# Attention heads in groups of three and two, maxima in the score stack, division in token rows

## The chip, the core and the metric

The kernel runs on one core of a Trainium2 chip. The core has TensorE (PE, with its weight loads shown as PEld), VectorE (DVE), ScalarE (ACT), GpSimd (POOL) and SyncE (SP, which here only issues DMAs). The metric is the device time of one execution in microseconds (us), the median of several runs.

## The reference, cut to what matters

Two layers over 4 sequences of 512 tokens of width 128. Each layer is a gated cross-attention (16 heads of width 8, 77 keys, context of the same sequence) and then a gated mixture of 8 experts (layer 0 picks one expert, layer 1 two). Layer 0 rotates queries and keys, layer 1 has biases and a mask on the keys.

```python
q = (x @ Wq).reshape(B, Nq, H, hd).transpose(0, 2, 1, 3)      # H = 16, hd = 8
attn = jax.nn.softmax(jnp.einsum('bhqd,bhkd->bhqk', q, k) * scale, axis=-1)
out = jnp.einsum('bhqk,bhkd->bhqd', attn, v).transpose(0, 2, 1, 3).reshape(B, Nq, C) @ Wo + bo
...
x = x + jnp.tanh(g_xattn[0]) * _L0_xattn_ref(_layernorm(x, axis=-1), ctx_1024, ...)
x = x + jnp.tanh(g_ffn[0]) * _L0_ffn_ref(_layernorm(x, axis=-1), ...)
x = x + jnp.tanh(g_xattn[1]) * _L1_xattn_ref(_layernorm(x, axis=-1), ctx_1024, ctx_1024, mask_SxS2_ik0, ...)
x = x + jnp.tanh(g_ffn[1]) * _L1_ffn_ref(_layernorm(x, axis=-1), ...)
```

## The kernel before

**Order.** Every engine runs its own program, and each walks the same list of steps k (`STEPS`) for each layer; a stage of batch b is due at step 12 b + `AT[stage]` (`due`). Within a step the order of the calls is the order of the engine's loop. A batch has 12 score tiles (`NS`), so batch b's scores are at steps 12 b to 12 b + 11. The maxima of batch b come in steps -12 to -3 relative to its first score, so they run during the scores of batch b - 1; its division, projection, second normalisation and routing come in steps 13 to 35, so during the scores of later batches. The front of a batch (statistics, normalisation, projection of the queries) comes in steps -30 to -19, that of batch 1 at 6 instead of 12 steps after that of batch 0 (`SECOND_FRONT`). After the steps of a layer follow `plan` and the expert tiles (24 and 40 tiles of 128 rows, L813 to L846 on PE).

**Attention.** Heads go in 4 groups of 4. Queries and keys are split in a high and a low half so that one single-pass float32r matmul gives their product: a stack of 128 rows holds high and low queries (`qs`, L342) against high and low keys (`ks`). 32 rows of dimensions carry 4 heads; the keys of one head are zero in the rows of the other heads, so `ks` has 4 x 77 = 308 columns for a group and batch.
- `spread_q` (L332, SP): 16 DMAs a batch that copy 32 rows of `qhl` into rows of `qs`, after `qh_ok` and `ql_ok` (the high and low half, L516 on ACT and L1020 on DVE). Three `qs` buffers rotate.
- `scores_for_max` (L718, PE): 16 units a batch, one per group and tile of 128 tokens, token rows against 308 keys; in layer 1 a mask matmul first (L730). Results go through a ring of 3 PSUM banks that other small results share. `maxima` (L1022, DVE) reduces each unit to 4 negated maxima.
- `split_max` (L1028) splits the maxima in high and low, `augmenting` (L733) transposes them, `copy_augT` (L518, ACT) takes them out of PSUM.
- `scores` (L737, PE): 12 tiles a batch of 103 or 102 key rows x 512 tokens: one matmul of queries and keys (L750) and one that adds the negated maxima and, in layer 1, the mask (L751). `exps` (L524, ACT) writes the exponentials to `probs`; two PSUM banks alternate.
- `weigh` (L753, PE): three times a batch, after 4 tiles: 4 matmuls of values into `ps_n` and 4 of ones into `ps_d`, plain float32, each with 32 output rows.
- Division: copies of `ps_d` and `ps_n` (L535, L536, ACT), `den_to_tokens` (4 transposes), `recip_den` (DVE), `widen_rd` (L538, ACT), `rden_to_dims` (4 transposes), `weigh_out` (L1049, DVE), then `output` (L777, PE) and `residual`.
- Keys, for both layers during layer 0: `spread_keys` (L673, PE) stacks the halves in 4 pairs of matmuls over 2 PSUM banks, `take_keys` copies each out (two on ACT, two on DVE), `mask_keys` writes the 4 heads from the copies. Layer 1's keys are spread at step `LAST + 24`, one step ahead of the router of batch 3.

## Time and profile before

| | us |
|---|---|
| median of 3 runs | 451.59 |
| lowest and highest run | 450.32, 460.82 |
| span of the profiled execution | 464.2 |
| PE busy (share of the span) | 314.7 (68%) |
| DVE busy | 264.1 (57%) |
| ACT busy | 136.3 (29%) |
| POOL busy | 152.2 (33%) |

The profile is one execution, and longer than the median by 12.6 us, so durations below come from it and sums are made against its span. Layer 0's attention fills about 10 to 160 us, its expert tiles 160 to 210, layer 1's attention 210 to 365, its tiles 365 to 447, and the end adds the results. The granted clock of TensorE is given as a share of 2.4 GHz; it is either 1.2 or 2.4 GHz at any moment, and a share between is a mean of the two over the stretch. A row with "x4" merges four instructions in a row.

### The profile page before, as it was taken

The page shows a single profiled execution, that of the slowest core. Times are in us where ns is not written, and L with a number is a line of the kernel's source. Part 1 is how long each engine was busy: PE and PEld are TensorE (multiplying, and loading weights), DVE is VectorE, ACT ScalarE, POOL GpSimd, SP SyncE. Part 2 cuts the span into 40 slices and gives each one's busy share as a digit, 9 for nine tenths or more (in the row PEclk, how much of TensorE's full clock was granted, in tenths as well). Part 3 has the DMA queues.
Part 4 walks back from the last instruction along what each step waited for, and adds up shares of the span by engine and source line. Part 5 has one row for each costly group of instructions (what it writes and reads, how often), then busy time and mean ns, then how long its engine had stood idle before and what let it go on. Part 6 is the DMA issues. An engine that isn't in the chain of part 4 may idle for free.

```text
span 464.2 us, 7008 instructions
## 1 busy us (share of the span) xinstructions
PE 314.7 (68%) x1932; PEld 228.1 (49%) x1932; DVE 264.1 (57%) x916; ACT 136.3 (29%) x302; POOL 152.2 (33%) x172
## 2 busy tenths in 40 slices
PE   2468999989754095751467999999530298888920
PEld 2236555545353094640256566654320297777820
DVE  2768668773675244353367667765545066665634
ACT  2412354535313033220103454354200033333300
POOL 3211212051423134561102102165766134555550
PEclk9767799999985579795567999999855599999985
DMA  7434032100000867823231313000103677988708
GB/s 268 126 74 118 12 80 52 43 11 19 17 8 29 224 215 215 243 73 90 62 85 36 71 27 85 14 24 23 42 29 100 213 244 236 299 249 289 235 12 269
DMA packets 39997, 52.93 MB, mean 114 GB/s; under 512 B 7177, under 2 KB 24334, under 8 KB 39968
## 3 DMA queue, kind: packets, MB, share of 16 engines
q1 hardware_dynamic: 33648, 45.03, 33.7%
q0 software_dynamic: 3584, 6.36, 3.9%
q10 hardware_dynamic: 2736, 1.20, 0.9%
q8 instruction: 13, 0.21, 0.2%
q14 instruction: 16, 0.13, 0.1%
HBM read 35.58 MB, written 9.64 MB: 97 GB/s over the span
## 4 chain that ended last, share of the span: by engine, by line
PE 21%; DVE 8%; issue 7%; DMA 6%; SPq 4%; POOL 4%; ACT 1%; POOLq 0%; DVEq 0%; ACTq 0%
POOL routed L445 3%; PE ps_s L750 2%; PE ps_a L730 2%; DMA xt<-routed 2%; PE ps_a L731 2%; PE ps_s L821 2%; SPq L342 2%; PE ps_s L751 2%; PE ps_t L705 2%; PE ps_n L765 2%; PE ps_a L838 1%; PE ps_d L765 1%; PE ps_t L821 1%; DMA probs<-expert_out 1%; DMA routed<-pay,slot 1%
## 5 line engine op out<-in xcount | busy, mean ns | idle before, releaser
L463 POOL DMA_INDIRECT expert_out<-yo,rows_at x64 | 63.0, 984 | 81.5 <-DVE yo L1179 63.6
L529 ACT ACTIVATE probs<-ps_s 103x512 f32<-103x512 f32 (+1 forms) x96 | 56.3, 597 | 56.8 <-PE ps_s L751 53.3
L445 POOL DMA_INDIRECT routed<-pay,slot x48 | 48.4, 1009 | 58.3 <-DVE slot L1132 47.8
L1025 DVE TENSOR_REDUCE negm<-ps_a 128x4 f32<-128x308 f32 x128 | 55.1, 470 | 19.5 <-PE ps_a L731 18.0
L750 PE MATMUL ps_s<-qs,ks 128*103 128x512 f32 (+1 forms) x96 | 46.2, 481 | 2.0 <-ACT augT L522 1.2
L731 PE MATMUL ps_a<-ks,qs 128*128 128x308 f32 x128 | 43.1, 374 | 5.9 <-DVE negm L1025 5.6
L421 POOL TENSOR_SCALAR ve<-mv 128x4 f32<-128x4 f32 x16 | 4.0, 251 | 116.0 <-DVE mv L975 116.0
L751 PE MATMUL ps_s<-augT,aug 128*103 128x512 f32 (+1 forms) x96 | 39.6, 412 | 0.0
L838 PE MATMUL ps_a<-cst,xt 128*128 128x128 f32 x32 | 11.1, 355 | 39.8 <-DMA xt<-routed 38.2
L731 PEld LDWEIGHTS ps_a<-ks,qs 128*128 128x128 f32 x128 | 28.9, 227 | 15.4 <-DVE negm L1025 6.6
L821 PE MATMUL ps_s<-xT,probs 128*128 128x128 f32 x208 | 32.5, 299 | 2.9 <-DVE xT L1190 1.7
L821 PEld LDWEIGHTS ps_s<-xT,probs 128*128 128x128 f32 x208 | 28.6, 210 | 4.1 <-DVE xT L1190 2.2
L750 PEld LDWEIGHTS ps_s<-qs,ks 128*103 128x103 f32 (+1 forms) x96 | 16.9, 177 | 25.0 <-issue 19.4
L730 PE MATMUL ps_a<-aug,maskT 128*128 128x308 f32 x64 | 23.5, 372 | 4.8 <-DVE negm L1025 4.8
L838 PEld LDWEIGHTS ps_a<-cst,xt 128*128 128x128 f32 x32 | 5.1, 159 | 43.6 <-DMA xt<-routed 39.3
L705 PE MATMUL ps_t<-cst,nrm 128*128 128x128 f32 x32 | 7.7, 386 | 27.1 <-DVE nrm L980 27.1
L765 PE MATMUL ps_n<-probs,vb 103*32 103x512 f32 (+1 forms) x192 | 25.6, 605 | 0.0
L765 PE MATMUL ps_d<-probs,cst 103*32 103x512 f32 (+1 forms) x192 | 25.0, 592 | 0.0
L1162 DVE SCALAR_TENSOR_TENSOR qr<-qr,ps_s 128x256 f32<-128x256 f32 x20 | 8.4, 420 | 27.8 <-ACT qr L600 19.0
L1190 DVE COPY xT<-ps_a 128x128 f32<-128x128 f32 x24 | 6.9, 291 | 30.4 <-PE ps_a L838 17.6
L610 ACT ACTIVATE xT<-ps_a 128x128 f32<-128x128 f32 x40 | 11.1, 278 | 36.0 <-PE ps_a L838 26.8
L705 PEld LDWEIGHTS ps_t<-cst,nrm 128*128 128x128 f32 x32 | 5.7, 199 | 28.9 <-DVE nrm L980 20.6
(168 smaller groups left out, 659.3 us busy)
## 6 DMA issues: line engine op xcount, KB each, us to landing
probs<-f_in SPq DMA_DIRECT2D x40, 384.0 KB
qs<-qhl SPq DMA_DIRECT2D x128, 64.0 KB, 2.0
probs<-f_in SPq DMA_DIRECT2D x24, 321.0 KB
xt<-routed SPq DMA_DIRECT2D x32, 65.0 KB
probs<-routed SPq DMA_DIRECT2D x32, 65.0 KB
yin<-expert_out SPq DMA_DIRECT2D x8, 256.0 KB, 4.4
routed<-pad ACTq DMA_DIRECT2D x18, 65.0 KB
x<-x_in SPq DMA_DIRECT2D x4, 256.0 KB, 7.6
```

Source lines behind the costliest of these rows:

```text
L445: pool.indirect_dma_start(out=routed[l], out_offset=bass.IndirectOffsetOnAxis(ap=slot[c][:, t:t + 1], axis=0), in_=pay[c][:, t, :], in_off ...
L463: pool.indirect_dma_start(out=expert_out[l], out_offset=bass.IndirectOffsetOnAxis(ap=rows_at[i % SHORT][:, :], axis=0), in_=yo[i % SHORT][ ...
L529: nc.scalar.activation(probs[n % 2][0:KSIZE[j], s, :], ps_s[(NS * n + s) % SCORE_BANKS][0:KSIZE[j], :], ACT.Exp, scale=SCALE).then_inc(exp ...
L705: last = nc.tensor.transpose(ps_t[:, i * P:(i + 1) * P], src(i), ident)
L730: nc.tensor.matmul(bank[:, 0:GK], maskT[:, i * P:(i + 1) * P], aug[:, g, :], start=True, stop=False)
L731: nc.tensor.matmul(bank[:, 0:GK], qs[n % 3][:, g, i * P:(i + 1) * P], ks[:, g, b, :], start=not l, stop=True).then_inc(ring_full, 1)
L750: nc.tensor.matmul(bank, ks[:, g, b, lo:hi], qs[n % 3][:, g, :], start=True, stop=False)
L751: nc.tensor.matmul(bank, aug[:, g, lo:hi], augT[n % 2][:, :], start=False, stop=True).then_inc(sc_full, 1)
L765: last = nc.tensor.matmul(bank[32 * g:32 * g + 32, :], lhs(g), probs[n % 2][0:kk, j * GROUPS + g, :], start=j == 0, stop=j == KT - 1)
L821: last = nc.tensor.matmul(up_bank[i % SHORT][:, c * P:(c + 1) * P], fw[i][:, c * P:(c + 1) * P], xT[i % SHORT][:, :], start=True, stop=True)
L838: nc.tensor.transpose(ps_a[i % 2][:, 0:P], xt[i][:, 0:D], ident).then_inc(f_xtr[l], 1)
L1025: nc.vector.tensor_reduce(negm[:, i, g * HPG:(g + 1) * HPG], a[:, 0:GK].rearrange("p (h k) -> p h k", h=HPG), AX.X, ALU.max, negate=True). ...
```

## The change

Heads go in six groups, four of three heads and two of two.
- **Stack.** A stack is 96 rows (high and low halves, two copies), and six more rows carry the high and low maxima of the group's heads, so one matmul over 102 rows gives the shifted scores. `mark_heads` writes ones into `ks` once. In layer 1 a mask matmul (77 rows) goes first, as L751 is gone.
- **Queries.** `spread_q` issues 12 DMAs a batch, each writing both copies from a source read twice. `spread_max` is new: 6 DMAs a batch, after `copy_augT`, that bring the maxima from `augT` into rows 96 to 101 of `qs`. `scores` wait for them.
- **Maxima.** 12 units a batch, each two groups side by side in a bank (2 matmuls of 256 columns; in layer 1 a mask matmul of 512 columns first); a unit has 6 or 4 maxima. They end at step -6, the split moves from -3 to -5 and the transposes from -2 to -4.
- **Sums.** Score tiles are 116, 115 and 77 rows. A `weigh` is 4 matmuls: the denominators of three heads come out in the 8 columns that three heads leave free of 32; the fourth head of each four has its own tile.
- **Division.** Numerators and denominators are transposed to token rows (8 transposes), divided there on DVE (`divide`, 5 operations), transposed back (4), copied by ACT.
- **Keys.** `spread_keys` makes 6 pairs over the same 2 banks, and `take_keys` writes the masked heads from PSUM (3, 3 and 2 operations on each of ACT and DVE); `mask_keys` is gone.
- **Memory.** One `probs` of 16 tiles used as a ring replaces two of 12. POOL clears some new tiles at the start and sets constants in `vb`.

```diff
-GROUPS, HPG = 4, 4
+GROUPS, TRIPLES = 6, 4
+HPG = [3, 3, 3, 3, 2, 2]
...
-    "split": -3, "augment": -2, "weigh0": 5, "weigh1": 9, "weigh2": 13, "sums": 13, "den": 15, "widen": 15, "rden": 17,
+    "split": -5, "augment": -4, "weigh0": 5, "weigh1": 9, "weigh2": 13, "sums": 13, "den": 15, "rden": 17,
...
-MAX_UNITS = [1, 2, 2, 2, 1, 2, 2, 2, 1, 1]
+MAX_UNITS = [2, 2, 2, 2, 2, 1, 1]
...
                 for g in range(GROUPS):
+                    q0, count = HD * FIRST_HEAD[g], HD * HPG[g]
                     for half, ready in enumerate((qh_ok, ql_ok)):
                         if g == 0:
                             sp.wait_ge(ready, n + 1)
-                        for c in range(2):
-                            rows = 64 * c + 32 * half
-                            sp.dma_start(qs[n % 3][rows:rows + 32, g, :].bitcast(F32), qhl[half][32 * g:32 * g + 32, :].bitcast(F32)).then_inc(qspread[n % 3][g], 16)
+                        sp.dma_start(qs[n % 3][48 * half:48 * half + 2 * count, g, :].bitcast(F32),
+                                     bcast(qhl[half][q0:q0 + count, :].bitcast(F32), 1, 2)).then_inc(qspread[n % 3][g], 16)
...
+            def spread_max(n):
+
+                sp.wait_ge(augT_ok, n + 1)
+                for g in range(GROUPS):
+                    sp.dma_start(qs[n % 3][STACK:ROWS, g, :].bitcast(F32),
+                                 augT[n % 2][MAXIMA * g:MAXIMA * (g + 1), :].bitcast(F32)).then_inc(qspread[n % 3][g], 16)
...
             for l in range(LAYERS):
                 for b in range(NB):
                     spread_q(NB * l + b)
+                    if l == 0 and b == 0:
+                        mark_heads()
+                    if b:
+                        spread_max(NB * l + b - 1)
                     if l == 0 and b == 1:
                         sp.dma_start(w[1][:, :], w_in[1]).then_inc(ld_w[1], 16)
+                spread_max(NB * l + NB - 1)
                 load_tiles(l)
...
+                    for h in range(HPG[g]):
+                        last = nc.scalar.activation(ks_heads(g, h), ps_s[0][0:STACK, 0:NB * KEYS].rearrange("p (b k) -> p b k", b=NB),
+                                                    ACT.Copy, scale=hm[0:STACK, h:h + 1])
+                    last.then_inc(k_even, 1)
...
                 for g in range(GROUPS):
                     if g >= 2:
-                        pe.wait_ge((k_even, k_odd)[g % 2], 2 * l + 1)
+                        pe.wait_ge((k_even, k_odd)[g % 2], GROUPS // 2 * l + g // 2)
...
+                    nc.tensor.matmul(bank[:, :].rearrange("p (c k) -> p c k", c=2), maskT[0:KEYS, i * P:(i + 1) * P], bcast(aug[0:KEYS, :], 1, 2), start=True, stop=False)
+                for c in range(2):
+                    g = 2 * v + c
+                    if i == 0:
+                        pe.wait_ge(qspread[n % 3][g], 48 * (n // 3) + 32)
+                    last = nc.tensor.matmul(bank[:, c * AUG:(c + 1) * AUG], qs[n % 3][0:STACK, g, i * P:(i + 1) * P],
+                                            ks_group(g, b)[0:STACK, :], start=not l, stop=not l or c == 1)
+                last.then_inc(ring_full, 1)
...
+                if lo == 0:
+                    pe.wait_ge(qspread[n % 3][g], 48 * (n // 3 + 1))
...
-                nc.tensor.matmul(bank, ks[:, g, b, lo:hi], qs[n % 3][:, g, :], start=True, stop=False)
-                nc.tensor.matmul(bank, aug[:, g, lo:hi], augT[n % 2][:, :], start=False, stop=True).then_inc(sc_full, 1)
+                hi = lo + KSIZE[j]
+                if l:
+                    nc.tensor.matmul(bank, aug[0:KEYS, lo:hi], maskT[0:KEYS, :], start=True, stop=False)
+                nc.tensor.matmul(bank, ks_group(g, b)[:, lo:hi], qs[n % 3][0:ROWS, g, :], start=not l, stop=True).then_inc(sc_full, 1)
...
-                for bank, lhs in ((ps_n, lambda g: vb[0:kk, j, b, 32 * g:32 * g + 32]), (ps_d, lambda g: hmv[0:kk, j, :])):
-                    for g in range(GROUPS):
-                        last = nc.tensor.matmul(bank[32 * g:32 * g + 32, :], lhs(g), probs[n % 2][0:kk, j * GROUPS + g, :],
-                                                start=j == 0, stop=j == KT - 1)
+                bank = ps_n if j < 2 else ps_d
+                for i in range(QUADS):
+                    last = nc.tensor.matmul(bank[32 * i:32 * i + 32, :], vb[0:kk, j, b, 32 * i:32 * i + 32], prob(n, j * QUADS + i)[0:kk, :],
+                                            start=j != 1, stop=j != 0)
...
+                nc.vector.tensor_scalar(rd[:, :, 3], singles[:, :, HD], 1e-30, None, ALU.max)
+                link(nc.vector.tensor_scalar(rd[:, :, 0:3], triples[:, :, 24:27], 1e-30, None, ALU.max))
+                link(nc.vector.reciprocal(rd[:, :, :], rd[:, :, :]))
+                nc.vector.tensor_tensor(dst[:, :, 24:32], singles[:, :, 0:HD], bcast(rd[:, :, 3], 2, HD), ALU.mult).then_inc(ring_used, 1)
+                nc.vector.tensor_tensor(dst[:, :, 0:24].rearrange("p q (h d) -> p q h d", d=HD), triples[:, :, 0:24].rearrange("p q (h d) -> p q h d", d=HD),
+                                        bcast(rd[:, :, 0:3], 3, HD), ALU.mult).then_inc(s_dve, 1)
```

## Rows read from the trace of the kernel before

**Rows 1.** Windows, PE alone: stretch, its length, busy us (count), granted clock, DMA share, GB/s.

```profile
61.00:82.00 21.00, 20.32 (x124) 1.00 0.27 64
...
265.00:288.00 23.00, 22.07 (x144) 1.00 0.28 65
```

**Rows 2.** Windows, DVE alone, the first of these stretches.

```profile
61.00:82.00 21.00, 15.24 (x45) 1.00 0.27 64
```

**Rows 3.** Timeline, PE: first score matmuls of batches; start us, us, line, operation, idle before.

```profile
40.24 0.48 PE L750 MATMUL ps_s<-qs,ks 128*103 128x512 f32 x1
...
62.82 0.48 PE L750 MATMUL ps_s<-qs,ks 128*103 128x512 f32 x1 [0.28 <-ACT augT L522]
...
83.26 0.47 PE L750 MATMUL ps_s<-qs,ks 128*103 128x512 f32 x1
...
103.94 0.77 PE L750 MATMUL ps_s<-qs,ks 128*103 128x512 f32 x1
...
247.40 0.76 PE L750 MATMUL ps_s<-qs,ks 128*103 128x512 f32 x1 [0.69 <-ACT augT L522]
...
266.60 0.48 PE L750 MATMUL ps_s<-qs,ks 128*103 128x512 f32 x1 [0.28 <-ACT augT L522]
...
287.56 0.48 PE L750 MATMUL ps_s<-qs,ks 128*103 128x512 f32 x1
```

**Rows 4.** Timeline, SP's queue in four stretches: start, us, line, DMA, count.

```profile
55.99 10.01 SPq L342 DMA_DIRECT2D qs<-qhl  x16
...
74.39 10.45 SPq L342 DMA_DIRECT2D qs<-qhl  x16
...
159.39 0.33 SPq L357 DMA_DIRECT2D probs<-f_in  x1
...
258.00 10.02 SPq L342 DMA_DIRECT2D qs<-qhl  x16
```

**Rows 5.** DMA issues by form: KB each, median us from issue to landing.

```profile
qs<-qhl SPq DMA_DIRECT2D x128, 64.0 KB, 2.0
```

**Rows 6.** Timeline, PE, layer 0, at the full clock.

```profile
53.82 1.06 PE L765 MATMUL ps_n<-probs,vb 103*32 103x512 f32 x8
...
55.68 0.47 PE L750 MATMUL ps_s<-qs,ks 128*103 128x512 f32 x1
...
58.01 0.39 PE L751 MATMUL ps_s<-augT,aug 128*102 128x512 f32 x1
58.24 0.30 PE L731 MATMUL ps_a<-ks,qs 128*128 128x308 f32 x1
58.38 0.39 PE L750 MATMUL ps_s<-qs,ks 128*102 128x512 f32 x1
```

**Rows 7.** Timeline, DVE: three maxima in a row.

```profile
63.95 1.24 DVE L1025 TENSOR_REDUCE negm<-ps_a 128x4 f32<-128x308 f32 x3
```

**Rows 8.** Groups by line, shapes kept apart: busy us, mean ns, idle before, releasers.

```profile
L1052 DVE TENSOR_TENSOR att<-ps_t,nums 128x512 f32<-128x512 f32 x8 | 5.5, 686 | 0.6 <-PE ps_t L705 0.6
...
L1047 DVE RECIPROCAL rd<-rd 128x64 f32<-128x64 f32 x8 | 4.4, 553 | 0.3
...
L949 DVE COPY probs<-ps_s 128x308 f32<-128x308 f32 x4 | 1.9, 476 | 3.7 <-PE ps_s L685 3.7
...
L563 ACT ACTIVATE probs<-ps_s 128x308 f32<-128x308 f32 x4 | 1.7, 422 | 1.9 <-PE ps_s L685 1.9
```

**Rows 9.** Timeline, layer 0's tail: spreading layer 1's keys, the router of batch 3.

```profile
140.64 2.68 PE L685 MATMUL ps_s<-khl,select 128*128 128x308 f32 x8
...
143.12 1.71 PE L792 MATMUL ps_a<-w,nT 128*128 128x8 f32 x8
```

**Rows 10.** Timeline, layer 1's front: batch 1's high half, then two matmuls of the maxima.

```profile
235.62 0.63 ACT L516 ACTIVATE qhl<-qr 128x512 fp32r<-128x512 f32 x1 [6.18 <-DMA qs<-qhl]
...
242.46 0.46 PE L731 MATMUL ps_a<-ks,qs 128*128 128x308 f32 x1
...
242.72 0.46 PE L730 MATMUL ps_a<-aug,maskT 128*128 128x308 f32 x1
```

More of the change, by code:

```diff
@@ L31 @@
 HEADS, HD = 16, 8
-GROUPS, HPG = 4, 4
-GK = HPG * KEYS
-KT = 3
-KROWS = 103
-KSIZE = [min(KROWS, GK - KROWS * j) for j in range(KT)]
-NS = KT * GROUPS
+SLOT_HEADS, QUADS = 4, 4
+GROUPS, TRIPLES = 6, 4
+HPG = [3, 3, 3, 3, 2, 2]
+FIRST_HEAD = [0, 3, 6, 9, 12, 14]
+HEAD_ORDER = [4 * i + a for i in range(QUADS) for a in range(3)] + [4 * i + 3 for i in range(QUADS)]
+TK = 3 * KEYS + 1
+GK = [TK, TK, TK, TK, 2 * KEYS, 2 * KEYS]
+KS_AT = [NB * sum(GK[:g]) for g in range(GROUPS + 1)]
+STACK = 96
+MAXIMA = 6
+ROWS = STACK + MAXIMA
+KT = 3
+KROWS = 116
+KSIZE = [KROWS, 3 * KEYS - KROWS, KEYS]
+NS = KT * QUADS
+PROBS = 16
+AUG = 256
+UNITS = GROUPS // 2 * TPB
+KS_END = KS_AT[GROUPS] - GK[GROUPS - 1] + AUG
 SCALE = float(HD) ** -0.5
@@ L878, in _ @@
                         pe.wait_ge(s_masked, 1)
-                        transposes(lambda i: augt[1][:, i, :], mask_tr, maskT_ok, 1)
+                        if reader:
+                            pe.wait_ge(*reader[-1])
+                        reader.append((maskT_ok, 1))
+                        for i in range(TPB):
+                            last = nc.tensor.transpose(ps_t[0:KEYS, i * P:(i + 1) * P], maskf[:, i, :], ident)
+                        last.then_inc(mask_tr, 1)
                     for b in due("turn", k):
@@ L962, in set_up @@
+                    last.then_inc(k_odd, 1)
             def set_up():
@@ L1216, in _ @@
                     for b in due("den", k):
[L1217 to L1219 removed]
+                        divide(n0 + b)
                     for b in due("router", k):
```

308 lines of the change are left out of this document (164 added, 144 removed).

## The prediction

> **What bounds the kernel now.** I read the windows first, because shares over the whole span mix attention with expert tiles. In a warm stretch of layer 0's attention PE is busy for 20.32 of 21.00 us at granted clock 1.00, in layer 1 for 22.07 of 23.00 [rows 1]; DVE is busy for 15.24 of the first 21 [rows 2]. A busy PE is not PE at its peak, but here there is next to no gap to fill: batches 0 to 2 of each layer are bound by PE, with DVE some 5 us behind it. Next I marked where the first score matmul of each batch starts [rows 3]. I call the time from one to the next a stretch: 22.6, 20.4 and 20.7 us in layer 0 (batches 0, 1, 2), 19.2 and 21.0 in layer 1. Batch 3's stretch and what follows (layer 0: weigh, divide, project, route) is a chain of latencies, not PE's work. Third I read SP's queue, which the change gives new work. Spreading one batch's queries is 16 DMAs in 10.0 us, so 0.63 each, and it starts 15.8, 11.6 and 10.6 us after the stretch's first score [rows 4]; one lands 2.0 us after its issue [rows 5]. That is hidden today: the queries spread in batch b's stretch are those of batch b+2, first read in the next stretch.
>
> **PE's work per batch.** At the full clock a 512-column matmul occupies PE for 0.23 us (58.01 to 58.24) and a 308-column one for 0.14; one weigh, eight groups (four sums, four denominators), takes 1.86 (53.82 to 55.68) [rows 6]. A 256-column matmul lies below both; by columns it is 0.115. The maxima inside the stack remove L751 in layer 0: 12 x 0.23 = 2.8 us. In layer 1 the mask matmul replaces it, so nothing. The weigh halves, as the denominators ride in spare columns: 3 x 0.93 = 2.8. The maxima go from 16 x 0.14 = 2.2 to 24 x 0.115 = 2.8 in layer 0 (+0.5, rounded), from 16 x 0.28 = 4.5 to 12 x 0.46 = 5.5 in layer 1 (+1.0). Four more transposes add about 0.4 by columns. Sum: -4.7 us a batch in layer 0, -1.4 in layer 1. If PE stayed the bound this would be all, 24 us in eight batches.
>
> **DVE and ACT.** A maximum of 308 columns follows the last after 0.41 us [rows 7]. One of 462 costs between 0.41 (all of it start cost) and 0.62 (by columns); I take 0.57. A batch then needs 8 x 0.57 + 4 x 0.41 = 6.2 against 6.6. The division is five operations: two small clamps, the reciprocal of 0.55 and 512 columns of products in two pieces, against 0.69 in one [rows 8]; about 1.9 us against 1.5, and it now sits at step 3 before the rotation. So DVE keeps its 15 to 17 us, and with PE at 15 to 16 in layer 0 the two share the bound near 19 us a stretch. ACT's copy of the attended rows replaces the widening, shape for shape.
>
> **The new wait.** `spread_max` puts six DMAs between the transposed maxima and the scores. SP issues in program order, and there `spread_q` of batch b+2 stands ahead of `spread_max` of batch b+1. Both fall in the same stretch. So a next stretch can't begin before SP's start on the queries (H after the first score), 12 DMAs, one more, and the landing: H + 12 x 0.63 + 0.6 + 2.0 = H + 10.2. Behind that wait on PE stand all later matmuls, the next maxima among them, and so DVE. A query DMA now writes 48 rows rather than 32 from a source read twice. No row shows that form. The price lies between 0.33 (a weight load into 128 partitions, [rows 4]) and 0.63 x 48/32 = 0.95; I keep 0.63, since the load with four times the rows is the cheaper one, so rows don't set it, and this one is the same SBUF to SBUF kind.
>
> H hardly falls. The rotation waits for project (step 4) on PE and for DVE's list before it. In layer 0, stretch 1, PE saves 0.9 (weigh) and 5 x 0.23 before it; DVE gains 2.1 (ten maxima where there were eight: 8 x 0.57 + 2 x 0.41 against 3.3) and about 1. Bounds 9.5 and 14.8; I keep 11.6, as the two nearly cancel. In layer 1 PE has ten units of 0.46 instead of eight of 0.28 (+2.4): H about 12.7 in stretch 0 and 12.1 in stretch 1.
>
> **The sum, layer 0.** First scores: the key copies become three masks per PSUM bank, each of 0.42 (ACT) or 0.48 (DVE) as the 308-column copies [rows 8], which delays batch 1's front by 1.4; maxima -0.4, one copy less in the split -0.2, the DMA +2.6: +3.4 us. Stretch 0: DVE works off values and statistics in those 3.4, so SP starts at 56.0 as before; 56.0 + 10.2 = 66.2 against 62.82: +3.4 in all. Stretch 1: 11.6 + 10.2 = 21.8 against 20.4: +4.8. Stretch 2 has no query spread in layer 0: 19.3 (DVE) against 20.7: +3.4; bounds 16.0 and 20.7. Batch 3 has no maxima after it: -2.9 (lighter weighs and scores on the chain): +0.5. Tail: today four key matmul pairs take 2.68 us and hold the router of batch 3 until 143.12 [rows 9]; with six pairs on two banks, each freed by three masks of 0.42 to 0.48, the router waits about 3.8 longer, in series on PE, while the lighter value products (-1.0) and the division against the weigh (-0.1) give back a little: +3.2. After the router comes the scatter that releases the tiles; nothing covers it.
>
> **The sum, layer 1.** Batch 1's high half waits 6.18 us for batch 0's query spread [rows 10]: four DMAs fewer, -2.5. `spread_max` +2.6. The maxima run there at 0.26 us per 308 columns (242.46 to 242.72): about even, 0. Stretch 0: 12.7 + 10.2 = 22.9 against 19.2: +3.7. Stretch 1: 12.1 + 10.2 = 22.3 against 21.0: +5.0. Stretch 2: -1.4 of PE, about +1 waiting for the landing: +4.6. Batch 3: -2.0: +2.6.
>
> **Clock.** The 0.26 against 0.14 is half of the full 2.4 GHz: PE had stood idle waiting for batch 1's front before it. With SP as the bound PE idles 3 to 4 us at the end of four stretches, so some of each next stretch should run at 1.2 GHz. I charge 1.6 us to each of the two stretches 1, bounds 0 and 3.3: +3.2. The Trainium skill (TensorE: Matmul & The Clock Gate, section "HAM oscillation") says that gaps between bursts put the throttle back and each burst then starts cold, which speaks against any change that thins PE's work out; the slow row agrees, and by its strict reading all four stretches would pay, as the clock rival below works out.
>
> Total 3.2 + 2.6 + 3.2 = +9.0. The profiled execution spans 464.2 us, 12.6 over the median of 451.59 of the runs shown, so the sum gives 473.2 there and 460.5 in the timed runs.
>
> **Rivals.** (a) *SP doesn't bind.* If a query DMA issues in 0.33 as the weight load does, H + 6.3 lies under what PE and DVE need, and stretches fall to 20.0, 19.3 and 19.3 in layer 0, 18.8 and 20.3 in layer 1. Then layer 0 gives +3.1, -2.6, -1.1, -1.4, -2.9, +2.7 = -2.2 and layer 1 -3.6 (front), -0.4, -0.7, -0.4, -2.0 = -7.1: 442.3. It decides below about 0.44 us a DMA (11.6 + 13 x 0.44 + 2.0 = 19.3). For it: 0.33 exists on this queue. Against: all spreads of the trace keep 0.63. (b) *Wide DMAs cost by rows*, 0.95: eight of twelve pay 0.32 more, 2.6 in each of four stretches and in layer 1's front, +13: 473. For: no row shows a source read twice; against: the weight load. (c) *The clock falls in every stretch that SP bounds*: 4 x 3.3 in place of 3.2: 470. For: the slow front of layer 1. Against: 20.32 us of PE in 21 held 1.00, and scattered work may hold it too. (d) *PE's relief in full*, -24 us less the front and tail costs of +6: 434; against it stands DVE's 15 us and the wait itself.
>
> **Numbers.** Forecast 0.55 (452 to 468 by the bounds of H), (a) 0.20, (b) 0.12, (c) 0.09, (d) 0.04. About 2%, 9 us, is what a measurement of this kernel tells from no change: 442.6 and 460.6 are the edges. The forecast lies on the upper edge, so half of it is no change and half slower; (a) is half faster, half no change; (b) and (c) slower, (d) faster. Faster 0.14, within 0.38, slower 0.48. The range is 444 to 472: it leaves out (d), half of (a) and little of (b).
>
> **What would show it.** Right: on SP's timeline the six maxima DMAs of batch b+1 stand directly behind twelve query DMAs without a gap, and the first score of the next batch waits for a DMA; weigh rows of 0.93; stretches near 22 us in layer 0's batch 1 and layer 1's 0 and 1, but under 20 in layer 0's batch 2; granted clock below 1.00 inside attention; the router of layer 0's batch 3 some 4 us later behind its keys. Wrong: query DMAs well under 0.5 us each, first scores that wait for ACT or nothing, stretches of 17 to 19 us everywhere.

## The result and the profile after

The changed kernel takes 508.41 us against 451.66, each the median of 4 runs. The ratio is 1.129 with an interval of 1.124 to 1.133; like all ratios below it leaves out runs in a slower state, into which some runs of either kernel fall. Its profiled execution spans 506.8 us. The forecast of 460.5 and its range to 472 missed by far, on the side that held the larger chance.

First, what to compare with. The profile of before spans 464.2 us, 12.6 over the median of its runs. I profiled that kernel once more (`before_again`, 452.6 us): the lengths of its stretches in the two layers repeat within 0.1 us, and all of the 12 us lie in the expert tiles and behind them (3.4 us between layer 0's batch 3 and layer 1's first score, 8.1 behind layer 1's stretches). So the stretches of [rows 3] stand, and for the tail and the tiles I use the second profile.

Windows of the kernel after, all engines, one line for each of the six stretches that end with the first score of another batch (stretch; its length; busy us of PE, PEld, DVE, ACT, POOL; granted clock; DMA share; GB/s), layer 0 first:

```profile
43.50:69.70 26.20, 16.24 (x75) 9.55 (x73) 15.41 (x45) 8.42 (x15) 5.04 (x6) 0.82 0.27 64
69.70:98.10 28.40, 21.03 (x97) 13.46 (x97) 14.53 (x36) 10.47 (x19) 3.79 (x4) 0.74 0.19 41
98.10:124.00 25.90, 20.57 (x102) 13.77 (x102) 16.17 (x50) 9.10 (x17) 5.98 (x6) 0.70 0.04 11
273.40:298.90 25.50, 19.76 (x87) 13.76 (x87) 12.72 (x34) 8.41 (x15) 1.27 (x3) 0.77 0.22 44
298.90:329.10 30.20, 26.40 (x118) 17.95 (x118) 14.64 (x37) 10.71 (x19) 3.12 (x4) 0.77 0.18 38
329.10:356.90 27.80, 25.95 (x126) 18.27 (x126) 16.49 (x62) 9.19 (x17) 4.74 (x6) 0.75 0.03 9
```

The same of the second profile of before, stretches 0 and 1 of each layer:

```profile
40.20:62.70 22.50, 19.43 (x94) 11.36 (x92) 15.95 (x47) 8.30 (x15) 4.94 (x6) 0.85 0.21 57
62.70:83.20 20.50, 19.21 (x121) 11.23 (x121) 15.72 (x43) 10.52 (x19) 3.91 (x5) 1.00 0.26 60
...
243.90:263.10 19.20, 18.89 (x98) 13.06 (x98) 12.81 (x35) 8.11 (x15) 3.39 (x5) 0.84 0.18 42
263.10:284.10 21.00, 20.38 (x135) 13.31 (x135) 15.15 (x44) 10.49 (x19) 3.27 (x5) 1.00 0.26 60
```

Read length and clock together. The stretches 1 and 2 of before took 20 to 21 us at clock 0.98 to 1.00; the first of each layer ran at 0.85 and 0.84, which the two warm windows of [rows 1] do not show. After has 25 to 30 us at 0.70 to 0.82 in all six. PE's busy time did not fall by 4.7 us a batch in layer 0; it rose in places, because busy time is time and each matmul at half clock counts longer.

SP's queue after (start, us, line, DMA, count), the answer to [rows 4]: layer 0's stretches 0 and 1, layer 1's 0 and 1.

```profile
58.21 9.40 SPq L369 DMA_DIRECT2D qs<-qhl  x12
67.65 4.32 SPq L384 DMA_DIRECT2D qs<-augT  x6
86.37 9.61 SPq L369 DMA_DIRECT2D qs<-qhl  x12
...
287.64 9.16 SPq L369 DMA_DIRECT2D qs<-qhl  x12
296.84 4.32 SPq L384 DMA_DIRECT2D qs<-augT  x6
317.89 9.16 SPq L369 DMA_DIRECT2D qs<-qhl  x12
327.09 4.32 SPq L384 DMA_DIRECT2D qs<-augT  x6
```

The first scores (PE's timeline), the answer to [rows 3]; in brackets how long PE was idle and what ended it:

```profile
43.52 0.46 PE L817 MATMUL ps_s<-qs,ks 102*116 102x512 f32 x1
...
69.70 0.78 PE L817 MATMUL ps_s<-qs,ks 102*116 102x512 f32 x1 [5.42 <-DMA qs<-augT]
...
98.06 0.78 PE L817 MATMUL ps_s<-qs,ks 102*116 102x512 f32 x1 [3.09 <-DMA qs<-augT]
...
298.89 0.78 PE L816 MATMUL ps_s<-maskT,aug 77*116 77x512 f32 x1 [4.78 <-DMA qs<-augT]
...
329.14 0.49 PE L816 MATMUL ps_s<-maskT,aug 77*116 77x512 f32 x1 [1.52 <-DMA qs<-augT]
```

The maxima's DMAs stand behind the queries' without a gap, and the first score waits for a DMA, as the prediction said it would look. The other rows that matter are the transposes of the normalised rows ahead of layer 0's batch 3, a score in the middle of a stretch at either clock, a weigh at either clock, and batch 3's router:

```profile
72.54 1.94 PE L833 MATMUL ps_d<-probs,vb 77*32 77x512 f32 x8
...
79.53 0.78 PE L817 MATMUL ps_s<-qs,ks 102*115 102x512 f32 x1
...
84.33 1.06 PE L833 MATMUL ps_n<-probs,vb 116*32 116x512 f32 x8
85.32 0.49 PE L817 MATMUL ps_s<-qs,ks 102*115 102x512 f32 x1
...
123.19 1.11 PE L760 MATMUL ps_t<-cst,pay 128*128 128x128 f32 x4 [3.20 <-DVE pay L1057]
...
162.89 1.11 PE L760 MATMUL ps_t<-cst,pay 128*128 128x128 f32 x4 [2.50 <-DVE pay L1057]
...
169.52 1.71 PE L865 MATMUL ps_a<-w,nT 128*128 128x8 f32 x8
```

After the 5.42 us of idle time at 69.70 the granted clock is half (1.2 GHz) until 81 us, so for 11 us in which PE has work: 0.78 for a score where 0.49 is the full clock's, 1.94 for a weigh where 1.06 is. Layer 0's third stretch has no query spreading in it, and its end waits for something else, 3.20 us for normalised rows.

Where the 54.2 us between the two profiles (452.6 and 506.8) went, beside the terms of the prediction:

| stretch | before | after | change | forecast |
|---|---|---|---|---|
| start to layer 0's first score | 40.16 | 43.52 | +3.4 | +3.4 |
| layer 0, stretch 0 | 22.6 | 26.2 | +3.6 | 0.0 |
| stretch 1 | 20.4 | 28.4 | +7.9 | +1.4 |
| stretch 2 | 20.7 | 25.9 | +5.2 | -1.4 |
| batch 3, tail, tiles, layer 1's front | 140.0 | 149.4 | +9.4 | -0.1 |
| layer 1, stretch 0 | 19.2 | 25.5 | +6.4 | +3.7 |
| stretch 1 | 21.0 | 30.2 | +9.3 | +1.3 |
| stretch 2 | 20.9 | 27.7 | +6.8 | -0.4 |
| batch 3 to the end | 147.6 | 149.9 | +2.3 | -2.0 |
| clock, charged apart | | | | +3.2 |
| sum (before rounding +54.2; the forecast put it at +9.0) | | | +54.3 | +9.1 |

So 39 of the 54 us lie in the six stretches.

### The profile page after: what moved, and what is told of

It reads as the page before. It is cut to its first block, busy times and chain, and to the rows that moved or that the text cites. A ratio compares the mean times of both kernels' runs of the same rounds, so it can differ in the third digit from the quotient of the medians.

```text
span 506.8 us, 6754 instructions
## 1 busy us (share of the span) xinstructions
PE 329.1 (65%) x1780; PEld 246.8 (49%) x1780; DVE 265.7 (52%) x898; ACT 138.1 (27%) x312; POOL 155.0 (31%) x178
## 4 chain that ended last, share of the span: by engine, by line
PE 18%; DMA 10%; SPq 7%; DVE 6%; issue 4%; POOL 4%; ACT 1%; POOLq 0%; DVEq 0%; ACTq 0%
SPq L369 5%; DMA xt<-routed 4%; PE ps_a L784 3%; PE ps_a L789 3%; POOL routed L504 3%; PE ps_s L894 2%; DMA probs<-expert_out 2%; PE ps_s L816 2%; PE ps_t L760 1%; PE ps_s L817 1%; DMA qs<-augT 1%; PE ps_d L833 1%; DMA routed<-pay,slot 1%; SPq L400 1%; DMA probs<-routed 1%
## 5 line engine op out<-in xcount | busy, mean ns | idle before, releaser
L1105 DVE TENSOR_REDUCE negm<-ps_a 128x6 f32<-128x462 f32 (+1 forms) x96 | 53.3, 581 | 52.0 <-PE ps_a L789 50.1
L596 ACT ACTIVATE probs<-ps_s 116x512 f32<-116x512 f32 (+2 forms) x96 | 54.9, 593 | 82.2 <-PE ps_s L817 82.0
L789 PEld LDWEIGHTS ps_a<-ks,qs 96*128 96x128 f32 x192 | 50.4, 287 | 15.1 <-DVE negm L1105 5.8
L789 PE MATMUL ps_a<-ks,qs 96*128 96x256 f32 x192 | 51.6, 387 | 4.5 <-DVE negm L1105 4.5
L817 PE MATMUL ps_s<-qs,ks 102*116 102x512 f32 (+2 forms) x96 | 47.0, 506 | 10.0 <-DMA qs<-augT 8.5
L817 PEld LDWEIGHTS ps_s<-qs,ks 102*116 102x116 f32 (+2 forms) x96 | 19.1, 207 | 26.8 <-issue 14.8
L816 PE MATMUL ps_s<-maskT,aug 77*116 77x512 f32 (+2 forms) x48 | 24.9, 519 | 9.6 <-DMA qs<-augT 9.1
L784 PE MATMUL ps_a<-aug,maskT 77*128 77x512 f32 x48 | 27.7, 578 | 3.4 <-DVE negm L1105 3.4
L1057 DVE TENSOR_SCALAR pay<-x,mv,rstd 128x128 f32<-128x128 f32 x32 | 15.3, 545 | 10.6 <-POOL rstd L474 10.4
L816 PEld LDWEIGHTS ps_s<-maskT,aug 77*116 77x116 f32 (+2 forms) x48 | 9.3, 194 | 23.6 <-issue 10.8
L760 PE MATMUL ps_t<-cst,pay 128*128 128x128 f32 x32 | 7.3, 367 | 20.1 <-DVE pay L1057 20.1
```

The source lines that it names most:

```text
L596: nc.scalar.activation(prob(n, s)[0:KSIZE[j], :], ps_s[(NS * n + s) % SCORE_BANKS][0:KSIZE[j], :], ACT.Exp, scale=SCALE).then_inc(exp_ok, 1)
L760: last = nc.tensor.transpose(ps_t[:, i * P:(i + 1) * P], src(i), ident)
L784: nc.tensor.matmul(bank[:, :].rearrange("p (c k) -> p c k", c=2), maskT[0:KEYS, i * P:(i + 1) * P], bcast(aug[0:KEYS, :], 1, 2), start=Tru ...
L789: last = nc.tensor.matmul(bank[:, c * AUG:(c + 1) * AUG], qs[n % 3][0:STACK, g, i * P:(i + 1) * P], ks_group(g, b)[0:STACK, :], start=not ...
L816: nc.tensor.matmul(bank, aug[0:KEYS, lo:hi], maskT[0:KEYS, :], start=True, stop=False)
L817: nc.tensor.matmul(bank, ks_group(g, b)[:, lo:hi], qs[n % 3][0:ROWS, g, :], start=not l, stop=True).then_inc(sc_full, 1)
```

## The experiments

Two theories stood at the start. **A**: SP's queue delays the first score, the idle time lets PE's clock fall, and that is the loss. **B**: PE's lighter work alone lets the clock fall. While the runs came in a third was added, **C**: PE, which walks a fixed list of steps, stalls on the next result that is late. Ratios are to runs of the kernel before on the same chip. Its medians beside these runs were 451.0 to 454.6, so between two changed versions a difference of 2 or 3 us says nothing.

### before_again: the kernel before, once more

> The kernel before once more, for a second profile. The one shown spans 464.2 us and the other runs lie near 451.6; either the missing 12.6 us lie in the attention (stretches of layer 1 at a granted clock under 1.00: then a second profile has layer 1's first stretches shorter, and the costs of attention in the kernel after are larger than the two profiles show), or in the expert tiles, and then all stretches of attention repeat within 0.5 us: 22.6, 20.4, 20.7 and 19.2, 21.0, 20.9.

452.6 us in the profile. Stretches 22.6, 20.4, 20.7 and 19.2, 21.0, 20.9: the attention repeats, the difference is the tiles'.

### max_on_act: the maxima's DMAs on another queue

`spread_max` leaves SP's loop and stands in ScalarE's, behind its copy of the transposed maxima.

```diff
                         copy_augT(n0 + b)
+                        spread_max(n0 + b)
```

> The kernel after, with the six DMAs of the maxima issued from ScalarE's queue right behind its copy of the transposed maxima, so that nothing of the query spreading stands ahead of them. Theory A (SP's queue delays the first score, and the idle time that this makes is what lets the clock fall): first scores no longer wait for a DMA by more than 1 us, the granted clock of the attention stretches goes from 0.70 to 0.82 back to 0.95 or more, stretches fall from 26 to 30 us to 20 to 22, about 38 us in all, total 465 to 475 us. Theory B (PE's lighter work alone lets the clock fall, the wait is incidental): the clock stays at 0.70 to 0.80 and stretches stay at 25 us or more, total 495 to 508.

504.66 us, 1.116 (1.105 to 1.128). Neither theory had this. ScalarE's timeline, and a score on PE's:

```profile
61.41 4.66 ACTq L584 DMA_DIRECT2D qs<-augT  x6
66.12 1.08 ACT L593 ACTIVATE probs<-ps_s 77x512 f32<-77x512 f32 x2 [4.74 <-issue]
```

```profile
93.29 0.46 PE L815 MATMUL ps_s<-qs,ks 102*77 102x512 f32 x1 [4.32 <-ACT probs L593]
```

Six issues hold ScalarE for 4.66 us, the exponentials behind them are late, and PE waits for those, 3.3 to 4.3 us a stretch, with the same clock after it (0.84 and 0.69 in layer 0's stretches 1 and 2). The wait moved to another engine's queue.

### keep_busy: matmuls in the wait

```diff
+KEEP = 14
...
+                bank = ps_s[k % SCORE_BANKS][0:KSIZE[j], :]
+                if s == 0 and b:
+                    pe.wait_ge(exp_ok, k - SCORE_BANKS + 1)
+                    for _ in range(KEEP):
+                        nc.tensor.matmul(bank, ks_group(0, b)[0:STACK, 0:KSIZE[j]], qs[(n - 1) % 3][0:STACK, 0, :], start=True, stop=True)
                 if lo == 0:
                     pe.wait_ge(qspread[n % 3][g], 48 * (n // 3 + 1))
```

> The kernel after, with 14 matmuls of 512 columns (3.2 us at the full clock) into the score bank just ahead of the wait for the first maxima of batches 1 to 3; their results are written over. The wait and SP's queue stay as they are; only PE is not idle in it. Theory A1 (most of the loss is the clock that falls in the wait and stays low for half of the next stretch): clock of the stretches 0.90 or more, stretches 22 to 24 us, total 480 to 490 us. Theory A2 (most of the loss is SP's queue itself): stretches stay within 1 us of 26, 28 and 26 in layer 0 and 25, 30 and 28 in layer 1, total 503 to 515.

496.70 us, 1.099 (1.084 to 1.114): 12 us back for more work. Between the two theories: where the fill covered the wait the clock held and the stretch got shorter (layer 1's stretch 1, the second line of these windows, 30.2 to 25.3); layer 0's stretch 1, which still began behind 3.0 us of idle time, stayed at 28 (the first line):

```profile
69.00:97.00 28.00, 23.22 (x110) 15.05 (x110) 14.54 (x36) 10.47 (x19) 3.77 (x4) 0.83 0.20 41
...
293.20:318.50 25.30, 22.98 (x132) 15.87 (x133) 14.28 (x37) 10.50 (x19) 3.12 (x4) 1.00 0.22 46
```

The first score of that second stretch, and SP's queue in it:

```profile
293.15 0.49 PE L821 MATMUL ps_s<-maskT,aug 77*116 77x512 f32 x1 [1.07 <-DMA qs<-augT]
```

```profile
305.82 9.15 SPq L370 DMA_DIRECT2D qs<-qhl  x12
315.01 4.32 SPq L385 DMA_DIRECT2D qs<-augT  x6
```

With the clock at 1.00 SP starts on the queries 12.7 us after the first score (305.82 - 293.15), where the kernel after has 19.0 and the forecast had 12.1. In layer 0's stretch 1, whose clock was not held, it starts after 16.4, against 16.7.

### before_plus_wait: the wait alone, in the kernel before

```diff
+            def spread_max(n):
+                sp.wait_ge(augT_ok, n + 1)
+                for g in range(6):
+                    sp.dma_start(xT[0][6 * g:6 * g + 6, :], augT[n % 2][6 * g:6 * g + 6, 0:P].bitcast(F32)).then_inc(mspread[g], 16)
...
                     spread_q(NB * l + b)
+                    if b:
+                        spread_max(NB * l + b - 1)
...
+                if s < 6:
+                    pe.wait_ge(mspread[s], 16 * (n + 1))
```

> The kernel before with nothing of the change but its wait: after ScalarE's copy of the transposed maxima SP issues six DMAs of 6 rows x 128 columns into an idle tile, in the same place of its queue (behind the query spreading of the next but one batch), and score tiles 0 to 5 of a batch wait for one each. Theory A (the wait behind SP's queue makes the loss, whatever the rest of the change does): first scores wait for a DMA, stretch >= 11.6 + 16 x 0.63 + 0.7 + 2.0 = 24 us, the clock falls below 0.90, total 480 to 495 us. Rival (PE's 20 us of work in a stretch hide most of it): stretches under 22.5 us, total under 465.

479.05 us, 1.060 (1.048 to 1.072): theory A, 27 us for the wait with nothing else changed. The six stretches sum to 143.8 us against 124.8. Their clock, expected under 0.90, is so in three of them (0.80 to 0.89) and 0.93 to 0.96 in the others. SP's timeline and the first score behind it:

```profile
54.00 10.06 SPq L343 DMA_DIRECT2D qs<-qhl  x16
64.11 4.67 SPq L349 DMA_DIRECT2D xT<-augT  x6
```

```profile
65.96 0.72 PE L762 MATMUL ps_s<-qs,ks 128*103 128x512 f32 x1 [5.42 <-DMA xT<-augT]
```

PE's heavier work in that kernel did not hide it. The 27 us are about half of the loss.

### no_max_spread2: the changed kernel without the wait

```diff
-                    if b:
-                        spread_max(NB * l + b - 1)
...
-                spread_max(NB * l + NB - 1)
...
-                    pe.wait_ge(qspread[n % 3][g], 48 * (n // 3 + 1))
+                    pe.wait_ge(qspread[n % 3][g], 32 * (n // 3 + 1))
```

> The kernel after without the DMAs of the maxima: this leaves out the subtraction of the maxima (rows 96 to 101 of the stacks stay zero); the maxima, their transposes and their copy are still computed. The price of the new wait and its DMAs, whole. Theory A (the wait is the loss, and PE has work without it): no first score waits, granted clock 0.95 or more in the attention stretches, stretches 19 to 22 us, total 455 to 470 us. Theory C (with the wait gone PE stalls on the next latency, the normalised rows of the batch before, for which it waits 2.3 to 3.2 us at the end of a stretch in the kernel after, and the clock falls there as well): stretches 23 to 25 us, clock 0.80 to 0.90, total 475 to 490 us.

482.23 us, 1.064 (1.055 to 1.073), as theory C expected. GpSimd clears the rows that the DMAs would have filled, and that start-up work holds the first query spreading (it starts at 22.27 us, at 16.99 in the kernel after), so 5 of these us belong to the experiment: without the wait the kernel would be near 477 (an estimate). So the wait costs 31 us by the medians, 34 by the ratios, and the rest of the change some 25. Windows of layer 0's stretches 1 and 2, then PE's waits over the attention of both layers (us in total, times, longest):

```profile
69.20:90.20 21.00, 16.25 (x96) 9.89 (x97) 14.42 (x36) 10.11 (x19) 3.77 (x4) 0.97 0.31 63
90.20:114.90 24.70, 19.93 (x104) 14.03 (x102) 16.19 (x50) 9.59 (x18) 5.95 (x6) 0.71 0.07 15
```

```profile
PE ps_t L751 <- DVE pay L1048: 15.1, 7, 3.6
PE ps_t L790 <- DVE augt L1108: 7.2, 7, 1.9
```

The first of the two stretches is the prediction's relief laid bare: 16.25 us of PE's work instead of 19.21, at nearly the full clock, and still 21.0 us long. PE waits for the normalised rows of the batch before (15.1 us in all; 10.0 in the second profile of before) and for the split maxima (7.2; before has one such wait, 1.4). Both sums leave out layer 1's last wait for normalised rows, 5.0 us in each profile.

### before_thin: PE's relief alone, in the kernel before

```diff
-                nc.tensor.matmul(bank, ks[:, g, b, lo:hi], qs[n % 3][:, g, :], start=True, stop=False)
-                nc.tensor.matmul(bank, aug[:, g, lo:hi], augT[n % 2][:, :], start=False, stop=True).then_inc(sc_full, 1)
+                last = nc.tensor.matmul(bank, ks[:, g, b, lo:hi], qs[n % 3][:, g, :], start=True, stop=not l)
+                if l:
+                    last = nc.tensor.matmul(bank, aug[:, g, lo:hi], augT[n % 2][:, :], start=False, stop=True)
+                last.then_inc(sc_full, 1)
...
-                    for g in range(GROUPS):
+                    if j == 1 and bank is ps_n:
+                        continue
+                    for g in range(1 if j == 1 else GROUPS):
```

> The kernel before with PE's relief of the change and nothing else: layer 0's second score matmul (L751) left out, so that the maxima are not subtracted there, and the middle weigh of a batch reduced from eight groups to one, so that numerators and denominators lack the keys of the middle score tiles. PE's work falls by 12 x 0.23 + 7 x 0.23 = 4.4 us a batch in layer 0 and 1.6 in layer 1; no wait is added and every other engine keeps its list. Theory P (rival (d): PE's relief counts in full): stretches 16 us in layer 0, total 428 to 434 us. Theory D (DVE and the chain of the division bind just below): stretches of 19 to 20 at clock 0.95 or more, total 440 to 448. Theory B (PE with gaps loses its clock and nothing is gained): clock under 0.90 in at least three stretches, total 450 to 465.

455.59 us, 1.016 (1.008 to 1.024): not faster. In its profile (450.4 us) the six stretches sum to 117.7 us against 124.8, so 7 of the 18 us that PE was spared there; waits grew (13.4 us for normalised rows where there were 10.0, 4.5 for the split maxima where there were 1.4). Layer 0's stretch 1:

```profile
60.00:79.40 19.40, 16.19 (x94) 9.03 (x95) 15.61 (x43) 10.46 (x19) 4.99 (x6) 1.00 0.29 68
```

16 us of PE's work, clock 1.00, 19.4 us long: the stretch fell by 1.0 us of the 4.4 that PE was spared, as theory D of the expectation had it for the stretches (not for the total, which it put at 440 to 448). No stretch is under clock 0.90, so lighter work by itself did not lower it. What holds the stretch stands in PE's timeline, the transposes of the normalised rows at the end of layer 0's stretch 1, in the second profile of before, in no_max_spread2 and here:

```profile
82.77 0.66 PE L705 MATMUL ps_t<-cst,pay 128*128 128x128 f32 x4 [1.08 <-DVE pay L980]
...
89.46 1.12 PE L751 MATMUL ps_t<-cst,pay 128*128 128x128 f32 x4 [2.26 <-DVE pay L1048]
...
79.01 0.66 PE L705 MATMUL ps_t<-cst,pay 128*128 128x128 f32 x4 [1.31 <-DVE pay L984]
```

They start 20.0, 20.3 and 19.0 us after the stretch's first score (62.74, 69.20, 60.05), however much work PE has. Before had 1.08 us of idle time there already. That the total is not shorter lies in part behind the attention of layer 0 (144.0 us from batch 3's first score to layer 1's, against 140.0), where other outputs route other tokens; I did not separate that.

### filled and no_max_filled: holding the clock with work

```diff
+                for _ in range(1 if l else 2):
+                    nc.tensor.matmul(bank, ks_group(0, b)[0:STACK, 0:KSIZE[j]], qs[n % 3][0:STACK, 0, :], start=True, stop=True)
                 hi = lo + KSIZE[j]
```

> The kernel after with filling matmuls of 512 columns into score banks, written over by the scores: 14 ahead of the wait for the first maxima of batches 1 to 3 (as in keep_busy), and 2 ahead of every score tile of layer 0, 1 of layer 1. PE gets 12 x 2 x 0.23 = 5.5 us more work a batch in layer 0, 2.8 in layer 1, and waits stay as they are. Theory B (PE's work became so thin that the clock falls, and that is a large part of the loss): clock 0.92 or more in every stretch, layer 0's stretches 24 to 25, 24 to 25 and 22 to 23 us, total 480 to 490, under keep_busy's 496.7 though PE has more to do. Rival (clock is not it): the added 33 us of work show, total 505 or more.

> no_max_spread2 (which leaves out the subtraction of the maxima) with 2 filling matmuls ahead of every score tile of layer 0 and 1 of layer 1, and layer 1's keys spread one step later, behind the router of batch 3. Theory B: clock 0.95 or more in every stretch, stretches 21 to 22 us, those of layer 0's batch 2 and layer 1's batch 0 about 2 us shorter than in no_max_spread2 (24.7 and 23.9); the router of layer 0's batch 3 starts 4 us after the transposes of its rows no longer but about 1; total 465 to 473 us. Rival (PE is busy enough without): stretches grow by the added work, 3 to 5 us each, total 490 or more.

503.62 us (1.121, 1.113 to 1.129) and 481.60 us (1.071, 1.062 to 1.082). Theory B loses in both. Without the wait the filling does hold the clock at 0.99 to 1.00 in layer 0's three stretches, and stretch 2 falls from 24.7 to 22.5 us, but stretch 1 rises from 21.0 to 22.1 and layer 1's stretches 0 to 2 stay between 23.3 and 24.1; the six sum to 135.7 against 136.7 (counted, here and in no_max_late, from the first matmul of queries and keys, in layer 1 0.3 to 0.6 us behind the mask's matmul of the table above). The later spreading of layer 1's keys moved batch 3's router forward, to 1.8 us behind the transposes of its rows from 6.6, but not the ranks behind it: 10.4 us behind them, against 10.2.

### after_late: the normalised rows two steps later

```diff
-    "output": 18, "stats2": 19, "normalise2": 23, "turn2": 23, "router": 25, "route_exp": 26, "ranks": 28,
-    "scatter0": 29, "scatter1": 31, "scatter2": 34, "scatter3": 35,
+    "output": 18, "stats2": 19, "normalise2": 23, "turn2": 25, "router": 27, "route_exp": 28, "ranks": 30,
+    "scatter0": 31, "scatter1": 33, "scatter2": 36, "scatter3": 37,
```

> The kernel after with the transposes of the normalised rows two steps later (step 25 for 23, router, ranks and scatters two later as well), so that they stand behind the first two score tiles of the next batch. Theory A (SP's queue sets the first score): layer 0's stretches 0 and 1 and layer 1's 0 and 1 keep their 25 to 30 us, only layer 0's stretch 2 (no query spreading in it) falls, from 25.9 to about 22; total 498 to 506. Theory C (waiting for the normalised rows is as large a part): every stretch falls by 2 to 4 us, total 485 to 495.

509.41 us, 1.126 (1.117 to 1.135). With the DMAs' wait in place the move is worth nothing: layer 0's stretch 2 falls as expected, 25.9 to 19.9 us, and layer 1's stretch 2 grows from 27.7 to 32.3:

```profile
321.20:353.50 32.30, 29.86 (x127) 21.07 (x126) 16.29 (x62) 9.65 (x18) 2.70 (x4) 0.65 0.02 5
```

### no_max_late: both fixed steps moved, no wait for DMAs

The edit of after_late in no_max_spread2, for all batches but the last (`LATE` names the stages from `turn2` to the scatters), and the transposes of the maxima a step later.

```diff
-    "split": -5, "augment": -4, "weigh0": 5, "weigh1": 9, "weigh2": 13, "sums": 13, "den": 15, "rden": 17,
+    "split": -5, "augment": -3, "weigh0": 5, "weigh1": 9, "weigh2": 13, "sums": 13, "den": 15, "rden": 17,
...
+    back = 2 if stage in LATE else 0
+    return [b for b in range(NB) if (SECOND_FRONT if b == 1 and stage in FRONT else NS * b) + AT[stage] - back * (b == NB - 1) == k]
```

> no_max_spread2 (which leaves out the subtraction of the maxima) with the two steps moved at which PE waits there: the transposes of the maxima one step later (-3 for -4) and those of the normalised rows, with router, ranks and scatters, two steps later for batches 0 to 2. Theory C (these waits, and the clock that they cost, are the rest of the loss): PE waits for normalised rows and split maxima shrink from about 13 to under 4 us over the attention, layer 0's stretch 2 falls from 24.7 to 20 to 21 us, layer 1's from 23.9, 22.7, 23.6 to about 21 each, clock 0.95 or more, total 466 to 473. Rival (PE's thin work and DVE's list bind, whatever the order): stretches within 1 us of no_max_spread2's, total 479 to 484.

468.12 us, 1.038 (1.029 to 1.048): theory C. 14 us fewer than no_max_spread2 by the medians, 12 by the ratios, by order alone. Stretches 21.0, 18.3, 19.8 and 20.9, 20.0, 21.7, sum 121.8 against 124.8 in the kernel before. The two waits over the attention, to be set beside those above:

```profile
PE ps_t L753 <- DVE pay L1050: 9.5, 4, 3.9
...
PE ps_t L792 <- DVE augt L1110: 3.1, 4, 1.9
```

All of the 9.5 us lie behind the last stretch of a layer. Inside the six stretches the two waits fell from 13.2 us to 1.1, and the stretches from 136.7 to 121.8.

Less the 5 us of start-up it is 463, still 12 over before. In the profiles it is 8.7 over: the first score +3.3, layer 0's batch 3 to layer 1's first score +6.4 and the end +2.0, against -3.0 in the stretches.

### max_first: the two swapped in SP's queue

```diff
+                    if b > 1:
+                        spread_max(NB * l + b - 1)
                     spread_q(NB * l + b)
...
-                    if b:
-                        spread_max(NB * l + b - 1)
+                    if b == 1:
+                        spread_max(NB * l)
```

> The kernel after with the two in SP's queue swapped from batch 2 on: the six DMAs of the maxima of batch b+1 stand ahead of the twelve of the queries of batch b+2. Theory A (only the place in the queue counts): first scores start 1.3 + 0.7 us after the copy of the transposed maxima, so 20 to 23 us after the one before; the queries land 5 us later than now but early enough; total 480 to 490. Rival (the queue has too much to do between the split maxima and the next stretch in any order): the wait moves from the first score to the first maxima of batch b+2, whose queries are issued 4.3 us later, behind the maxima; PE stalls there by 4 us or more with the clock low, total 498 to 512.

514.55 us, 1.146 (1.134 to 1.157): the rival. The first score waits 0.38 us now, and the first maxima behind it wait for queries, here and, by PE's waits over the attention, 19.3 us in all:

```profile
64.45 0.46 PE L819 MATMUL ps_s<-qs,ks 102*116 102x512 f32 x1 [0.38 <-ACT probs L598]
69.10 0.55 PE L791 MATMUL ps_a<-ks,qs 96*128 96x256 f32 x1 [4.18 <-DMA qs<-qhl]
```

### pool_late: the maxima brought by copies

```diff
+                for g in (range(0, 4) if part == 0 else range(4, GROUPS)):
+                    at = 32 * (g % 4)
+                    nc.gpsimd.tensor_copy(qs[n % 3][STACK:ROWS, g, :], augT[part][at:at + MAXIMA, :].bitcast(F32)).then_inc(moved, 1)
+                    pool.wait_ge(moved, GROUPS * n + g + 1)
```

> The kernel after with both waits taken away: the maxima are transposed onto rows 0, 32, 64 and 96 (two transposes sets), copied out by ScalarE and brought into rows 96 to 101 by GpSimd copies in place of the six DMAs, and the normalised rows are transposed two steps later. All is computed. Theory A and C together: PE is not idle for more than 2 us at the end of a stretch, clock 0.95 or more, stretches 19 to 21 us, total 445 to 455 us. If PE's lighter work is itself what lets the clock fall (theory B): clock under 0.85, stretches 23 us or more, total 480 or more.

499.68 us, 1.100 (1.090 to 1.110). The expectation missed by 45 us. Timelines of GpSimd, DVE and PE in layer 0's stretch 1:

```profile
64.08 2.62 POOL L500 CAST qs<-augT 6x512 fp32r<-6x512 f32 x4
...
69.52 0.23 POOL L466 TENSOR_SCALAR ve<-mv 128x4 f32<-128x4 f32 x1
```

```profile
70.90 1.11 DVE L1073 TENSOR_SCALAR nrm<-x,mv,rstd 128x128 f32<-128x128 f32 x4 [7.21 <-POOL rstd L467]
```

```profile
72.62 0.80 PE L802 MATMUL ps_a<-ks,qs 96*128 96x256 f32 x2 [2.29 <-DVE negm L1121]
```

The copies hold GpSimd from 64 to 68 us, the power that the next batch's normalisation needs stands behind them, DVE is idle for 7.21 us, its maxima are late and PE waits 2.29 us for them; layer 0's stretch 1 takes 26.5 us at clock 0.74. By the total alone theory B would have it; these rows show another cause.

### before_late and before_late3: the same move in the kernel before

before_late has after_late's edit in the kernel before; before_late3 keeps batch 3 at the old steps.

> The kernel before with the transposes of the normalised rows two steps later (step 25 for 23; router, ranks and scatters two later as well). In layer 0 PE waits for these rows 1.1 us ahead of batch 2 and 2.0 us ahead of batch 3, whose first scores then run at half clock. If the wait and the clock it costs are what the move can give: 2 to 4 us shorter, 448 to 450 us. If steps of the tail are delayed by as much: no change, 452.

> before_late with batch 3, whose chain stands alone at a layer's end, left at its old steps. before_late shortened the stretches by 6.9 us in all (124.8 to 117.9) but lost some of it behind layer 1's keys in the tail. If the tail was the loss: 445 to 448 us, 0.985 to 0.99 of the kernel before. If the stretches' gain is given back elsewhere: 450 to 452.

450.30 us, 1.002 (0.998 to 1.007), and 452.61 us, 1.006 (1.002 to 1.009). In before_late's profile the six stretches sum to 117.9 us against 124.8, but 2.5 of these 6.9 us are layer 0's stretch 0 (20.1 us), which in before_late3, with the same move, kept 22.7. The timed runs show none of it, and no version that I ran beats the kernel before. Where the stretches' gain goes in the timed runs stays open.

## Why the prediction was wrong, point by point

**The shape of the wait was right.** It said that a stretch is H (SP's start on the queries) plus twelve query DMAs, one more and a landing. Measured in layer 0's stretch 0: 58.21 - 43.52 = 14.7, then 9.4, then 2.05 from the first maxima DMA's start to the score, 26.2 in all, which is the stretch. It holds to 0.1 us in all four stretches with query spreading.

**Its constant was a little low.** Twelve query DMAs took 9.16 to 9.61 us, 0.76 to 0.80 each where I kept 0.63. The landing came out: 2.05 us from the start of the issue is the 2.0 of [rows 5], which counts from the issue, so the 0.6 for "one more" was counted twice. Together 11.2 to 11.7 for 10.2: 5 us over four stretches. Bounds were 0.33 and 0.95; the value lies between the one kept and that of rival (b). The range's edge of 472 lay under (b)'s own 473, so it left out more of (b) than "little".

**H is the first step that failed.** "H hardly falls" gave 12.4 (56.0 - 43.6), 11.6, 12.7 and 12.1; measured 14.7, 16.7, 14.3 and 19.0, 16 us more in sum. I counted PE's and DVE's lists up to the rotation at the full clock. But behind the wait in front of a stretch the clock is half for 9 to 14 us, where project and the maxima lie, so PE reaches the rotation later, SP starts later, and the next wait comes again. 12 of the 16 us are in the two stretches 1, and keep_busy shows the cause there: with the clock held, H was 12.7 in layer 1's stretch 1 and not 19.0. The loop was the thing to see: wait, slow start, late queries, wait. Layer 0's stretch 0 has no wait in front of it; its 2.3 us go with gaps of 1.0 to 1.3 us inside it and a clock of 0.82, and were not tested apart.

**The clock is the second.** I charged 3.2 us, no more than 3.3 a stretch; neither 1.6 nor 3.3 was worked out from a row. Rival (c) had the mechanism (the clock falls wherever SP bounds) but the same price, and ended at 470. Measured: 0.70 to 0.82 in all six stretches, also in the two that SP doesn't bind. One 512-column matmul costs 0.43 there instead of 0.23 (0.63 against 0.40 in the records). Behind the idle times PE is busy at half clock for 9 to 14 us on end, so half of that, 4.5 to 7 us a stretch, is my estimate of the price, if all of that work would fit in half the time. The Trainium skill (TensorE: Matmul & The Clock Gate, section "HAM oscillation"), cited in the prediction for gaps that put the throttle back, is borne out by these rows, and its strict reading was the better guide than my discount.

**"DVE at 19.3" is the third, and the costliest.** For a stretch without SP's wait I put a length a little above the two busy sums (PE 15 to 16, DVE 15 to 17) that no row gives. Rival (a), in which SP doesn't bind, gave 442.3 on that footing and rival (d) 434. no_max_spread2 takes the wait away and lands near 477, 35 us above (a); the wait itself I had at 18 (460.5 - 442.3), and it measured 31 to 34. before_thin gives PE's relief and nothing else and gets 455.6. What binds below 20.5 us is neither engine's sum but the chain weigh, division, projection, normalisation, whose results PE awaits at fixed steps in the middle of its list; the change also moved the split of the maxima to step -5, where it stands on DVE right behind the residual of the batch before, and the transposes that wait for it to -4: 7.2 us of waits for 1.4. Each such wait stands in PE's order ahead of all later scores. no_max_late shows what they cost: 12 to 14 us from moving two steps. Whether the division in token rows makes the chain itself longer was not tested apart.

**Layer 0's tail** was right in its part and short in its sum: the router stands 169.52 - 162.89 = 6.6 us behind the transposes of its rows against 2.9 in the second profile of before (140.17 to 143.08), +3.7 for a forecast of +3.8. But batch 3's lighter weighs and scores gave back nothing (-2.9 in the sum): up to its last scatter, 55.0 us after its first score against 48.6, the clock was 0.62 against 0.82. **The front** was right in sum, +3.4; its terms were not read apart. The shares of the sum that were worked out from rows of one engine's issue order held; those that took work off PE and expected time for it did not.

**In sum**: the wait is 27 us in the kernel before and 31 to 34 in the changed one, shown by before_plus_wait and no_max_spread2; 12 to 14 of the rest are the fixed steps, shown by no_max_late; the last 12, front, tail and end, are read from rows and not tested apart. How much of each is idle time and how much clock I can't split: matmuls in the wait gave 12 us back (keep_busy), but filling all score tiles cost more than it gave.

## What to carry to other kernels

Before taking work off an engine that is busy for 95% of a stretch, list what each of its waits in that stretch would wait for if it came there earlier; the relief ends at the first of them, here after 1 us of 4.4. A transfer put between the last producer and the first consumer of a pipeline stage costs the queue in front of it too, and moving it to another engine's queue (max_on_act, pool_late) or up in its own (max_first) only chooses who is late. Where idle time also slows the engine that was idle, price a wait by the stretch that follows it, not by its length.
